# A graph network on one core: the spread of the last layer through all eight PSUM banks, with stores for two steps

## The chip, the cores and the metric

One Trainium2 chip, one of its cores. The metric is the time of one execution in device microseconds (us). A kernel is run several times and its median is given; one further execution is profiled.

## The reference

Four graph layers work on 12,500 nodes of 32 features and 400,000 edges (`src`, `dst`). After each one the features are `x = layernorm(x + layer(x))`. The layers are graph attention, a normalised partial convolution, a radial convolution with two spherical degrees, and a two-step graph convolution. The change concerns the last of them:

```python
def gcn_conv(x, W, b, row, col, n_nodes):
    xw = x @ W
    deg = segment_sum(ones, col); dinv = where(deg > 0, rsqrt(deg), 0)
    msgs = (dinv[row] * dinv[col])[:, None] * xw[row]
    return segment_sum(msgs, col, n_nodes) + b
...
h = relu(gcn_conv(x, W1, b1, row, col, n))      # row = src, col = dst, with a loop on each node
h = relu(gcn_conv(h, W2, b2, row, col, n))
```

So each of the two convolutions takes a row of 32 numbers per edge from its source node and adds it to its destination node.

## The kernel before

The node table lies in SBUF, 98 windows of 128 nodes. A gather of 400,000 single rows is avoided in this way. The edges are sorted by source, padded and cut into chunks of four edges. A **spread** multiplies a 0/1 matrix with the node table: for each edge slot its source row comes out, in three bf16 parts that sum to the fp32 row (3 x 32 = 96 columns for an edge, 384 for a chunk). The result goes to a DRAM table (`spread`) of chunks, 768 bytes each. Then a **collect** reads these chunks back in the order of the other end by indirect DMAs and sums them into the nodes. Layer 2 has a spread and a collect (k = 0, 34 features), the last layer has two of each (k = 1 and k = 2, 32 features), with small matrix products between them. Spread and collect follow each other: the collect reads what the spread wrote, anywhere in it.

A spread has 468 steps (`XSTEPS`), each of two groups of 128 chunks. The engines run their own loops and wait for each other by semaphores. For k = 1 and 2 a step n goes like this:

- SP loads the keys of four steps at once, 512 KB written to SBUF (4,096 bytes, the same ones, to each partition), into one of three key buffers (`key_load`).
- DVE makes the 0/1 matrix of the step, 128 x 1024 bf16, in `hotT` (`row_hot`, L2285). There are two such buffers; the matrix of step n + 2 waits until the matmuls of step n are done (`spread_raw`).
- PE runs eight matmuls of 96 columns (`spread_rows`, L1353) into two PSUM banks. Steps take turns between banks 0 and 1 and banks 2 and 3: step n waits until step n - 2 has been read (`spread_read`). PE's loop goes round every four steps, and each pair of steps loads its window numbers.
- ACT copies both banks as bf16 to one of four buffers in `srcs` (L1011), 1,536 bytes in a partition. It waits until the store of step n - 4 has landed (`spread_out`).
- SP stores the buffer, 128 runs of 1,536 bytes, 192 KB (L572). One queue, SP's, carries the key loads and the stores, in the order in which SP's program has them: the key load of a group of four stands ahead of the store of its fourth step.

Behind a spread, DVE clears the sums (L2311), and POOL begins the gathers of the collect once every store has landed. The chunk numbers by which it gathers are made long before, in `edge_list`, by shifts and masks: chunk (step n, partition p, group g) lies at row 256 n + 2 p + g.

For k = 0 the spread shares the copies between ACT and DVE, ACT's queue has the stores, and POOL gathers edge records meanwhile.

Of the kernel before, what the change touches and what calls it, by code (L numbers as in the profile page):

```python
# [7 lines left out]
BF16 = mybir.dt.bfloat16  # L8
I32 = mybir.dt.int32
U8 = mybir.dt.uint8  # L10
ALU = mybir.AluOpType
# [3 lines left out]
P = 128  # L15
# [17 lines left out]
SLOTS = 4  # L33
# [23 lines left out]
CHUNK_EDGES = 4  # L57
XTILES = CHUNK_EDGES
XGROUP = XTILES * P
XGPS = 2  # L60
XITERS = -(-((E + W * W * (CHUNK_EDGES - 1) + W * (XGROUP - CHUNK_EDGES)) // XGROUP) // (SLOTS * XGPS))
XSTEPS = XITERS * SLOTS
KEYS = 12
KEY_ITERS = XSTEPS // KEYS
RING = KEYS // SLOTS
assert KEY_ITERS * KEYS == XSTEPS and KEYS % SLOTS == 0
XG = XSTEPS * XGPS
XT = XG * XTILES
CHUNKS = XG * P
# [13 lines left out]
CHUNK_MASK = (1 << 17) - 1  # L83
# [74 lines left out]
def resnorm_gnn_kernel(nc, a, out):  # L158

    ctx = ExitStack()  # L160
    with ctx:
# [3 lines left out]
        def sem(name):  # L165
            return ctx.enter_context(nc.semaphore(name))
# [175 lines left out]
        def chunk_rows(s, c):  # L342
            size = XGPS * CHUNK_EDGES * 3 * c
            return srcs[:, s * size // 2:(s + 1) * size // 2].bitcast(BF16).rearrange("p (g c) -> p g c", g=XGPS)

        hotT_row = [hotT[:, b, :, :].rearrange("p t n -> p (t n)") for b in range(2)]

        yb = hot[:, :, :, :].rearrange("p b t n -> p (b t n)")[:, 0:2 * PW * P].rearrange("p (b w n) -> p b w n", b=2, w=PW)
# [53 lines left out]
        spread_read = sem("spread_read")  # L402
        spread_half = sem("spread_half")
        spread_out = [sem(f"spread_out{s}") for s in range(SLOTS)]
        nbx_in = [sem(f"nbx_in{r}") for r in range(RING)]
        chunks_in = [sem(f"chunks_in{s}") for s in range(SLOTS)]
        sq_in = sem("sq_in")
# [107 lines left out]
        def _(sp):  # L515
# [41 lines left out]

            def spread_moves(k, c, keys, rows):

                rows_v = rows.rearrange("(n p g) c -> p n g c", p=P, g=XGPS)  # L560
                keys_v = keys.rearrange("(m b) c -> m (b c)", b=SLOTS)

                def key_load(m, r):
                    sp.dma_start(row_keys_in[r], keys_v[bass.ds(m, 1), :].to_broadcast([P, SLOTS * XGPS * XGROUP])).then_inc(row_key_landed[r], 16)

                def step(i, s, final):
                    n = i * KEYS + s
                    if not final and s % SLOTS == SLOTS - 1:
                        sp.wait_ge(spread_hot, n + (k * XSTEPS + SLOTS + 1))
                        key_load(i * RING + (RING + s // SLOTS), s // SLOTS)  # L570
                    sp.wait_ge(spread_read, n + (k * XSTEPS + 3))
                    sp.dma_start(rows_v[:, bass.ds(n, 1), :, :],  # L572
                                 chunk_rows(s % SLOTS, c).rearrange("p (a g) c -> p a g c", a=1)).then_inc(spread_out[s % SLOTS], 16)

                for r in range(RING):
                    sp.wait_ge(spread_hot, k * XSTEPS + (SLOTS - KEYS + (r + 1) * SLOTS))
                    key_load(r, r)
                with sp.Fori(0, KEY_ITERS - 1) as i:
                    for s in range(KEYS):
                        step(i, s, False)  # L580
                for s in range(KEYS):
                    step(KEY_ITERS - 1, s, True)
# [97 lines left out]
            sp.wait_ge(row_keys_sent, 32)  # L680
            for s in range(SLOTS):
                sp.wait_ge(staged_out[s], 16 * ITERS)
                sp.wait_ge(spread_out[s], 16 * 3 * XITERS)

        N_LOADS = 18

# [2 lines left out]
        def _(pool):  # L689
# [99 lines left out]
                        gather_step(pas, i, s, False)  # L789

            def chunk_gather(k, pas, c, rows):
                for s in range(SLOTS):
                    pool.wait_ge(spread_out[s], 16 * XITERS * (k + 1))
                with pool.Fori(0, KEY_ITERS) as i:
                    for r in range(RING):
                        pool.wait_ge(nbx_in[r], i * 16 + (16 * k * KEY_ITERS + 16))
                        for s in range(SLOTS):
                            pool.wait_ge(sums_ready, i * KEYS + (SUMS_BASE[pas] + r * SLOTS + s + 1 - SLOTS))
                            pool.nop(nofuse=True)
                            for q in range(XGPS):  # L800
                                pool.indirect_dma_start(  # L801
                                    out=chunk_rows(s, c)[:, q, :], out_offset=None, in_=rows,
                                    in_offset=bass.IndirectOffsetOnAxis(ap=nbx[:, r, s * XGPS + q:s * XGPS + q + 1], axis=0),
                                ).then_inc(chunks_in[s], 16)
# [53 lines left out]
        def _(act):  # L858
# [136 lines left out]

            def spread_rows(k, c, keys, rows):
                c3 = 3 * c
                rows_v = rows.rearrange("(n p g) c -> p n g c", p=P, g=XGPS)
                keys_v = keys.rearrange("(m b) c -> m (b c)", b=SLOTS)

                def key_load(m, r):
                    act.dma_start(row_keys_in[r], keys_v[bass.ds(m, 1), :].to_broadcast([P, SLOTS * XGPS * XGROUP])).then_inc(row_key_landed[r], 16)

                def step(i, s, first, final):
                    n = i * KEYS + s
                    slot = s % SLOTS
                    act.wait_ge(spread_raw, n + (k * XSTEPS + 3))
                    if k or not first or s >= SLOTS:
                        act.wait_ge(spread_out[slot], i * (16 * KEYS // SLOTS) + 16 * (s // SLOTS + k * XITERS))
                    if k:  # L1010
                        s_.copy(chunk_rows(slot, c), banks[:, 2 * (s % 2):2 * (s % 2) + 2, 0:CHUNK_EDGES * c3]).then_inc(spread_read, 1)  # L1011
                        return
                    s_.copy(chunk_rows(slot, c)[:, 0, :], bank[2 * (s % 2)][:, 0:CHUNK_EDGES * c3]).then_inc(spread_read, 1)
                    act.wait_ge(spread_read, n + (k * XSTEPS + 3))
                    act.wait_ge(spread_half, n + 1)
                    act.dma_start(rows_v[:, bass.ds(n, 1), :, :],
                                  chunk_rows(slot, c).rearrange("p (a g) c -> p a g c", a=1)).then_inc(spread_out[slot], 16)
                    if not final and s % SLOTS == SLOTS - 1:
                        act.wait_ge(spread_hot, n + (k * XSTEPS + SLOTS + 1))
                        key_load(i * RING + (RING + s // SLOTS), s // SLOTS)  # L1020

                if k == 0:
                    for r in range(RING):
                        key_load(r, r)
                for s in range(KEYS):
                    step(0, s, True, False)
                with act.Fori(1, KEY_ITERS - 1) as i:
                    for s in range(KEYS):
                        step(i, s, False, False)
                for s in range(KEYS):  # L1030
                    step(KEY_ITERS - 1, s, False, True)
# [98 lines left out]
        def _(pe):  # L1130
# [209 lines left out]
            def spread_rows(k, c, win_tab):  # L1340
                c3 = 3 * c
                tabs = acc[:, 0:W * c3 // 2].bitcast(BF16)
                with pe.Fori(0, XITERS) as i:
                    for s in range(SLOTS):
                        n = i * SLOTS + s
                        if s % 2 == 0:
                            pair = group_windows(pe, PE_ENGINE, win_tab, i * (SLOTS // 2) + s // 2)
                        wins = pair[s % 2 * XGPS:(s % 2 + 1) * XGPS]
                        pe.wait_ge(spread_hot, n + (k * XSTEPS + SLOTS + 1))
                        pe.wait_ge(spread_read, n + (k * XSTEPS + 1))  # L1350
                        for q in range(XGPS):
                            for j in range(CHUNK_EDGES):
                                last = t_.matmul(bank[2 * (s % 2) + q][:, j * c3:(j + 1) * c3],  # L1353
                                                 hotT_row[s % 2][:, q * XGROUP + j:(q + 1) * XGROUP:CHUNK_EDGES],
                                                 tabs[:, bass.ds(wins[q] * c3, c3)], start=True, stop=True)
                        last.then_inc(spread_raw, 1)
# [89 lines left out]
        def _(dve):  # L1446
# [483 lines left out]
            def edge_list(k, ends, others, key_tab, numbers):  # L1930
# [17 lines left out]
                dve.drain()  # L1948
                wide = numbers.shape[1]
                low, high = [sortA[:, b * wide:(b + 1) * wide].bitcast(I32) for b in range(2)]  # L1950
                v.tensor_scalar(low, got, P - 1, 1, ALU.bitwise_and, ALU.logical_shift_left)
                v.tensor_scalar(high, got, CHUNK_MASK - (XGPS * P - 1), None, ALU.bitwise_and)
                v.tensor_scalar(numbers[:, :], got, 7, XGPS - 1, ALU.logical_shift_right, ALU.bitwise_and)
                dve.drain()
                v.tensor_tensor(low, low, high, ALU.bitwise_or)
                dve.drain()
# [308 lines left out]
            def spread_rows(k, c):  # L2265
# [33 lines left out]
                else:  # L2299
# [7 lines left out]
                            evict(i - 1 if s == 0 else i, (s - 1) % KEYS, False)  # L2307
                    evict(KEY_ITERS - 1, KEYS - 1, False)
                dve.wait_ge(spread_raw, (k + 1) * XSTEPS + 2)
                dve.drain()  # L2310
                v.memset(acc[:, 0:W * c3], 0.0)  # L2311
                dve.drain()
# [287 lines left out]
```

## Time and profile before

| | us |
|---|---|
| median of 3 runs (lowest, highest) | 19703.42 (19679.15, 19707.19) |
| the profiled execution | 19675.2 |
| its span, from first to last instruction | 19673.4 |
| spread k = 1, first matrix to last copy | 15917.7 to 16489.6 |
| spread k = 2, the same | 17838.8 to 18413.3 |

The profiled execution lies 28 us under the median and 4 us under the fastest of the three runs. Times in rows are from the span's start. Busy time is that of an engine's own work; "granted clock" (PEclk) is TensorE's, as a share of 2.4 GHz, and at any moment it is 0.50 or 1.00.

### The profile page before, as it was taken

The page shows a single profiled execution, that of the slowest core. Times are in us where ns is not written, and L with a number is a line of the kernel's source. Part 1 is how long each engine was busy: PE and PEld are TensorE (multiplying, and loading weights), DVE is VectorE, ACT ScalarE, POOL GpSimd, SP SyncE. Part 2 cuts the span into 40 slices and gives each one's busy share as a digit, 9 for nine tenths or more (in the row PEclk, how much of TensorE's full clock was granted, in tenths as well). Part 3 has the DMA queues.
Part 4 walks back from the last instruction along what each step waited for, and adds up shares of the span by engine and source line. Part 5 has one row for each costly group of instructions (what it writes and reads, how often), then busy time and mean ns, then how long its engine had stood idle before and what let it go on. Part 6 is the DMA issues. An engine that isn't in the chain of part 4 may idle for free.

```text
span 19673.4 us, 267135 instructions
## 1 busy us (share of the span) xinstructions
PE 9126.0 (46%) x63546; PEld 6808.2 (35%) x63547; DVE 16353.7 (83%) x22350; ACT 6238.3 (32%) x13799; POOL 12841.6 (65%) x13651
## 2 busy tenths in 40 slices
PE   0113101001016776603348887887888764327432
PEld 0113101001016665402235555555555543225322
DVE  9989999999998888816669999999999976665666
ACT  0001333333315553300015555555555553005200
POOL 0047777777777777777757777777777613760476
PEclk6556555555559997555568888888888855555555
DMA  1024444444422223713330000000001165245524
GB/s 19 0 56 31 32 34 32 33 30 32 33 26 59 48 48 87 244 31 84 84 39 13 13 13 13 13 13 13 13 13 13 12 174 177 79 72 196 159 79 69
DMA packets 1751554, 1095.95 MB, mean 56 GB/s; under 512 B 1217323, under 2 KB 1658124, under 8 KB 1750028
## 3 DMA queue, kind: packets, MB, share of 16 engines
q0 software_dynamic: 454272, 412.11, 17.5%
q1 hardware_dynamic: 1089532, 417.46, 8.5%
q10 hardware_dynamic: 207632, 265.14, 4.3%
q14 instruction: 84, 0.69, 0.0%
q8 instruction: 34, 0.56, 0.0%
HBM read 700.94 MB, written 391.12 MB: 56 GB/s over the span
## 4 chain that ended last, share of the span: by engine, by line
POOL 32%; DVE 25%; issue 16%; DMA 13%; DVEq 8%; PE 5%; ACT 1%; POOLq 0%; SPq 0%; ACTq 0%
POOL gat L779 16%; POOL pay L745 12%; DVE red L2504 12%; DMA srcs<-spread,nbx 9%; DVE srcs L2497 5%; DVEq L2503 4%; POOL srcs L801 4%; DMA spread<-srcs 3%; PE banks L1267 3%; DVE arena L1721 2%; DVE srcs L2493 2%; ACT srcs L1011 1%; DVEq L1791 1%; DVEq L2487 1%; PE banks L1353 1%
## 5 line engine op out<-in xcount | busy, mean ns | idle before, releaser
L779 POOL DMA_INDIRECT gat<-tab,nbr x3328 | 3330.8, 1001 | 2142.7 <-DMA nbr<-nbr_src 1128.6
L801 POOL DMA_INDIRECT srcs<-spread,nbx x2808 | 2655.2, 946 | 2305.0 <-DMA nbx<-from_src 1381.4
L779 POOL DMA_INDIRECT gat<-tab,pay x3328 | 3166.9, 952 | 1080.0 <-issue 816.2
L1411 PE MATMUL banks<-w2rows,dsts 128*128 128x384 f32 x6656 | 3030.9, 593 | 793.3 <-DVE srcs L2497 702.3
L745 POOL DMA_INDIRECT pay<-records,nbr x2560 | 2520.5, 985 | 795.3 <-issue 779.4
L1267 PE MATMUL banks<-srcs,hot 128*128 128x96 bf16 (+1 forms) x11232 | 1148.6, 279 | 2900.3 <-DMA srcs<-spread,nbx 2814.0
L2504 DVE TENSOR_REDUCE red<-srcs 128x160 f32<-128x2560 f32 x832 | 2346.3, 2820 | 75.8
L1196 PE MATMUL banks<-ident,arena 128*128 128x128 f32 x2240 | 429.8, 379 | 4206.5 <-DVE arena L1749 2792.2
L897 ACT COPY banks<-arena 128x1024 f32<-128x1024 f32 (+1 forms) x1508 | 1325.3, 880 | 2970.6 <-DVE arena L1749 1273.4
L2188 DVE TENSOR_TENSOR arena<-arena,banks 128x96 f32 (+2 forms) x2816 | 722.9, 257 | 1618.5 <-PE banks L1267 1344.0
L1267 PEld LDWEIGHTS banks<-srcs,hot 128*128 128x128 bf16 x11232 | 874.9, 134 | 3174.0 <-issue 1590.0
L1196 PEld LDWEIGHTS banks<-ident,arena 128*128 128x128 f32 x2240 | 404.1, 204 | 4232.7 <-DVE arena L1749 2802.5
L1411 PEld LDWEIGHTS banks<-w2rows,dsts 128*128 128x128 f32 x6656 | 1306.1, 218 | 1558.0 <-DVE srcs L2497 883.8
L2497 DVE TENSOR_TENSOR srcs<-banks,g_v 128x768 f32<-128x768 f32 x1664 | 1576.9, 948 | 0.0
L1748 DVE TENSOR_TENSOR arena<-banks,arena 128x1024 f32<-128x1024 f32 (+1 forms) x1508 | 1533.1, 1017 | 22.8 <-ACT banks L897 22.8
L1749 DVE TENSOR_TENSOR arena<-banks,arena 128x1024 f32<-128x1024 f32 (+1 forms) x1508 | 1532.8, 1016 | 0.0
L1353 PE MATMUL banks<-arena,hotT 128*128 x11232 | 1161.0, 282 | 757.5 <-DVE hotT L2285 347.2
L2285 DVE TENSOR_SCALAR hotT<-dsts,lanes 128x1024 bf16<-128x1024 uint8 x1404 | 1080.3, 775 | 447.4 <-PE banks L1353 426.7
L2493 DVE TENSOR_TENSOR srcs<-banks,g_s 128x512 f32<-128x512 f32 x1664 | 1142.1, 686 | 138.9 <-issue 63.2
L1353 PEld LDWEIGHTS banks<-arena,hotT 128*128 128x128 bf16 x11232 | 883.2, 139 | 1035.0 <-issue 1029.4
L1060 ACT COPY arena<-banks 128x57 f32 x1664 | 341.3, 205 | 2707.5 <-PE banks L1398 2682.1
L2177 DVE TENSOR_TENSOR hot<-banks,key_dst 128x1024 bf16<-128x1024 f32 x936 | 1141.2, 1219 | 38.6 <-issue 38.5
(383 smaller groups left out, 20253.1 us busy)
## 6 DMA issues: line engine op xcount, KB each, us to landing
spread<-srcs SPq DMA_DIRECT2D x936, 192.0 KB
dsts<-key_rows SPq DMA_DIRECT2D x234, 512.0 KB
spread<-srcs ACTq DMA_DIRECT2D x468, 204.0 KB
staged<-gat SPq DMA_DIRECT2D x416, 148.0 KB
gat<-staged ACTq DMA_DIRECT2D x416, 148.0 KB
dsts<-key_rows ACTq DMA_DIRECT2D x117, 512.0 KB
gat<-tab,nbr POOLq DMA_INDIRECT x3328
gat<-tab,pay POOLq DMA_INDIRECT x3328
```

What stands on the lines that cost most here:

```text
L745: pool.indirect_dma_start(out=pay[:, s, t, :], out_offset=None, in_=records, in_offset=bass.IndirectOffsetOnAxis(ap=nbr[:, s, t:t + 1], ax ...
L779: pool.indirect_dma_start(out=gatv(s, GC[pas])[:, t, :], out_offset=None, in_=TAB[pas], in_offset=bass.IndirectOffsetOnAxis(ap=row, axis=0 ...
L801: pool.indirect_dma_start(out=chunk_rows(s, c)[:, q, :], out_offset=None, in_=rows, in_offset=bass.IndirectOffsetOnAxis(ap=nbx[:, r, s * X ...
L897: s_.copy(sort_held(part, log, first), first).then_inc(operand_held, 1)
L1267: last = t_.matmul(where(q), hots[:, t, :], rows(t), start=(h == 0), stop=(h == tiles - 1))
L1353: last = t_.matmul(bank[2 * (s % 2) + q][:, j * c3:(j + 1) * c3], hotT_row[s % 2][:, q * XGROUP + j:(q + 1) * XGROUP:CHUNK_EDGES], tabs[:, ...
L1411: last = t_.matmul(bank[1 + 2 * (p % 2) + h][:, 0:384], hid_rows[:, s % 2, 2 * p + h, :], w2rows[:, :], start=True, stop=True)
L1748: v.tensor_tensor(b[:, d, e, :, :, :], held, a[:, d, 1, :, :, :], ALU.min)
L1749: last = v.tensor_tensor(b[:, d, 1 - e, :, :, :], held, a[:, d, 1, :, :, :], ALU.max)
L2493: v.tensor_tensor(prod[:, f0:f0 + 2, 0:16, :], banks[:, lo:lo + 2, 0:256].rearrange("p t (u k) -> p t u k", k=16), g_s[:, b, t0:t0 + 2, :] ...
L2497: v.tensor_tensor(prod[:, f0:f0 + 2, 16:40, :].rearrange("p t (o u) k -> p t o u k", o=3), banks[:, lo:lo + 2, 256:384].rearrange("p t (a ...
L2504: v.tensor_reduce(red[:, b, t0 - 2:t0 + 2, 0:40], prod[:, :, :, :], AX.X, ALU.add)
```

## The change

In the two spreads of the last layer (k = 1 and 2) the steps go round all eight PSUM banks, four pairs of them, so PE waits for the read of step n - 4 in place of n - 2. ACT copies into three pair buffers (`pair_rows`, in another part of SBUF, `acc`), each of which holds two steps: in a partition 3,072 bytes that follow each other. One store for two steps, 384 KB, takes the place of two stores of 192 KB. In DRAM the rows of two steps now lie side by side for a partition, chunk at row 512 (n // 2) + 4 p + 2 (n mod 2) + g, and `edge_list` makes chunk numbers for that, with as many instructions. The spread of k = 0 writes the same order of rows with its stores as they were, one for a step: 128 runs of 1,632 bytes, now 3,264 bytes apart. Before it clears the sums, DVE also waits for ACT's last copy. `hotT`, the key buffers and PE's loop stay as they are.

```diff
+PAIRS = 3
+SPREAD_DEEP = 4
+PAIR_USES = XSTEPS // 2 // PAIRS
...
+        def pair_rows(j, c):
+            size = 2 * XGPS * CHUNK_EDGES * 3 * c
+            return acc[:, 9600 + j * size // 2:9600 + (j + 1) * size // 2].bitcast(BF16).rearrange("p (a g c) -> p a g c", a=2, g=XGPS)
...
             def spread_moves(k, c, keys, rows):
-                rows_v = rows.rearrange("(n p g) c -> p n g c", p=P, g=XGPS)
+                rows_v = rows.rearrange("(n p a g) c -> p n (a g c)", p=P, a=2, g=XGPS)
...
-                    sp.wait_ge(spread_read, n + (k * XSTEPS + 3))
-                    sp.dma_start(rows_v[:, bass.ds(n, 1), :, :],
-                                 chunk_rows(s % SLOTS, c).rearrange("p (a g) c -> p a g c", a=1)).then_inc(spread_out[s % SLOTS], 16)
+                    if s % 2:
+                        j = s // 2 % PAIRS
+                        sp.wait_ge(spread_read, n + (k * XSTEPS + 3))
+                        sp.dma_start(rows_v[:, bass.ds(i * (KEYS // 2) + s // 2, 1), :],
+                                     pair_rows(j, c).rearrange("p a g c -> p (a g c)").rearrange("p (n c) -> p n c", n=1)).then_inc(pair_out[j], 16)
...
             def spread_rows(k, c, keys, rows):
                     act.wait_ge(spread_raw, n + (k * XSTEPS + 3))
-                    if k or not first or s >= SLOTS:
-                        act.wait_ge(spread_out[slot], i * (16 * KEYS // SLOTS) + 16 * (s // SLOTS + k * XITERS))
                     if k:
-                        s_.copy(chunk_rows(slot, c), banks[:, 2 * (s % 2):2 * (s % 2) + 2, 0:CHUNK_EDGES * c3]).then_inc(spread_read, 1)
+                        j, used = s // 2 % PAIRS, s // 2 // PAIRS + (k - 1) * PAIR_USES
+                        if s % 2 == 0 and (used or not first):
+                            act.wait_ge(pair_out[j], i * (16 * KEYS // 2 // PAIRS) + 16 * used)
+                        s_.copy(pair_rows(j, c)[:, s % 2, :, :], banks[:, 2 * (s % SPREAD_DEEP):2 * (s % SPREAD_DEEP) + 2, 0:CHUNK_EDGES * c3]).then_inc(spread_read, 1)
                         return
...
-                    act.dma_start(rows_v[:, bass.ds(n, 1), :, :],
+                    act.dma_start(rows_v[:, bass.ds(i * (KEYS // 2) + s // 2, 1), s % 2, :, :],
...
             def spread_rows(k, c, win_tab):
-                        pe.wait_ge(spread_read, n + (k * XSTEPS + 1))
+                        deep = SPREAD_DEEP if k else 2
+                        pe.wait_ge(spread_read, n + (k * XSTEPS + 3 - deep))
...
-                                last = t_.matmul(bank[2 * (s % 2) + q][:, j * c3:(j + 1) * c3],
+                                last = t_.matmul(bank[2 * (s % deep) + q][:, j * c3:(j + 1) * c3],
...
-                v.tensor_scalar(low, got, P - 1, 1, ALU.bitwise_and, ALU.logical_shift_left)
-                v.tensor_scalar(high, got, CHUNK_MASK - (XGPS * P - 1), None, ALU.bitwise_and)
-                v.tensor_scalar(numbers[:, :], got, 7, XGPS - 1, ALU.logical_shift_right, ALU.bitwise_and)
+                v.tensor_scalar(low, got, P - 1, 2, ALU.bitwise_and, ALU.logical_shift_left)
+                v.tensor_scalar(high, got, CHUNK_MASK - (2 * XGPS * P - 1), None, ALU.bitwise_and)
+                v.tensor_scalar(numbers[:, :], got, 7, 2 * XGPS - 1, ALU.logical_shift_right, ALU.bitwise_and)
...
                 dve.wait_ge(spread_raw, (k + 1) * XSTEPS + 2)
+                dve.wait_ge(spread_read, (k + 1) * XSTEPS + 2)
                 dve.drain()
                 v.memset(acc[:, 0:W * c3], 0.0)
```

The program orders of the two engines that the stores tie together show the change. First ACT, in its loop over twelve steps of a spread of the last layer, a few copies from the loop's start on (`srcs` and `arena` are where the copy writes; what a copy waits for stands behind it). Before:

```order
L1011 CAST srcs<-banks 128x768 [waits spread_out0]
L1007 REGISTER_ALU
L1011 CAST srcs<-banks 128x768 [waits spread_out1,spread_raw]
L1007 REGISTER_ALU
L1011 CAST srcs<-banks 128x768 [waits spread_out2,spread_raw]
L1007 REGISTER_ALU
L1011 CAST srcs<-banks 128x768 [waits spread_out3,spread_raw]
L1007 REGISTER_ALU
L1009 REGISTER_ALU [waits spread_raw]
L1011 CAST srcs<-banks 128x768 [waits spread_out0]
```

and now:

```order
L1030 CAST arena<-banks 128x768 [waits pair_out0]
L1025 REGISTER_ALU
L1030 CAST arena<-banks 128x768 [waits spread_raw]
L1025 REGISTER_ALU
L1030 CAST arena<-banks 128x768 [waits pair_out1,spread_raw]
L1025 REGISTER_ALU
L1030 CAST arena<-banks 128x768 [waits spread_raw]
L1025 REGISTER_ALU
L1030 CAST arena<-banks 128x768 [waits pair_out2,spread_raw]
L1025 REGISTER_ALU
L1030 CAST arena<-banks 128x768 [waits spread_raw]
```

Every copy waited for a store of its own slot; now every second one waits for the store of a pair, three pairs back.

Second SP, in the same loop, around a key load (`dsts` is the key buffer). Before:

```order
L572 ISA [waits spread_read]
L572 DMA spread<-srcs 128x768
L569 REGISTER_ALU
L564 ISA [waits spread_hot]
L564 DMA dsts<-key_rows 128x4096
L571 REGISTER_ALU
L572 ISA [waits spread_read]
L572 DMA spread<-srcs 128x768
L571 REGISTER_ALU
L572 ISA [waits spread_read]
L572 DMA spread<-srcs 128x768
```

and now:

```order
L584 ISA [waits spread_read]
L584 DMA spread<-arena 128x1536
L579 REGISTER_ALU
L574 ISA [waits spread_hot]
L574 DMA dsts<-key_rows 128x4096
L583 REGISTER_ALU
L584 ISA [waits spread_read]
L584 DMA spread<-arena 128x1536
L584 ISA [waits spread_read]
L584 DMA spread<-arena 128x1536
```

The key load stood ahead of the fourth store of four; it now stands ahead of the second of two, so it comes up in SP's program right behind the store of the first two steps, and the store that follows it waits for two more copies.

## Rows read from the trace of the kernel before

**Rows 1.** First spread, busy us of PE, PEld, DVE, ACT, POOL; PEclk, DMA share, GB/s.

```profile
15917.70:16489.60 571.90, 377.29 (x3744) 289.25 (x3744) 348.35 (x468) 362.60 (x468) 0.00 (x0) 0.50 0.79 265
```

**Rows 2.** ACT's copies (L1011), first spread, then second: durations, first and last start; idle before.

```profile
L1011 ACT CAST srcs<-banks x468: 798/798/809, 15919.5 to 16488.8; 128x768 bf16<-128x768 f32 x156
  DMA spread<-srcs: 118.2, 86
...
L1011 ACT CAST srcs<-banks x468: 798/798/809, 17840.7 to 18412.5; 128x768 bf16<-128x768 f32 x156
```

**Rows 3.** Who waited for whom, 15925 to 16480: us in total, times, longest.

```profile
PE banks L1353 <- ACT srcs L1011: 162.4, 213, 1.8
...
PE banks L1353 <- DVE hotT L2285: 2.6, 3, 1.0
```

**Rows 4.** The chain of waits, 15925 to 16480, by line.

```profile
by line: DMA spread<-srcs 60.2%; ACT srcs L1011 17.2%; PE banks L1353 12.3%; issue 6.4%; SPq L572 2.4%; SPq L564 1.4%; ACTq L1009 0.3%; SPq L571 0.1%; SPq L569 0.1%
```

**Rows 5.** The same chain in order of time, from 16201: start, us, what.

```profile
16201.93 4.36 DMA spread<-srcs
...
16206.36 0.81 ACT srcs L1011
...
16211.52 0.81 ACT srcs L1011
...
16212.49 2.93 DMA spread<-srcs
...
16221.55 4.31 DMA spread<-srcs
```

**Rows 6.** PE in order of time at the spread's start: start, us, [idle before <-releaser].

```profile
15918.67 1.48 PE L1353 MATMUL banks<-arena,hotT 128*128 x16 [43.84 <-DVE hotT L2285]
15920.52 1.49 PE L1353 MATMUL banks<-arena,hotT 128*128 x16 [0.36 <-ACT srcs L1011]
15922.62 1.47 PE L1353 MATMUL banks<-arena,hotT 128*128 x16 [0.61 <-ACT srcs L1011]
15924.47 1.49 PE L1353 MATMUL banks<-arena,hotT 128*128 x16 [0.39 <-ACT srcs L1011]
```

**Rows 7.** PE's weight loads and DVE's matrices in order of time, from 16201.

```profile
16201.89 0.61 PEld L1353 LDWEIGHTS banks<-arena,hotT 128*128 128x128 bf16 x8 [1.15 <-issue]
16202.76 0.75 DVE L2285 TENSOR_SCALAR hotT<-dsts,lanes 128x1024 bf16<-128x1024 uint8 x1 [1.02 <-PE banks L1353]
16203.74 0.62 PEld L1353 LDWEIGHTS banks<-arena,hotT 128*128 128x128 bf16 x8 [0.28 <-issue]
16205.23 0.62 PEld L1353 LDWEIGHTS banks<-arena,hotT 128*128 128x128 bf16 x8 [0.87 <-issue]
```

**Rows 8.** DMA queue of SP, 15925 to 16480: packets, MB, share of 16 engines; issues.

```profile
q1 hardware_dynamic: 81635, 148.69, 80.3%
spread<-srcs SPq DMA_DIRECT2D x454, 192.0 KB
```

**Rows 9.** The same queue, 15921.2 to 15923.1, in which two stores and nothing else move.

```profile
q1 hardware_dynamic: 288, 0.39, 58.3%
```

**Rows 10.** The same queue, 15875.1 to 15881.3, in which three key loads and nothing else move.

```profile
q1 hardware_dynamic: 432, 1.57, 68.5%
```

**Rows 11.** Busy time by engine in two stretches of the first spread, columns as in rows 1.

```profile
16166.00:16170.00 4.00, 2.98 (x32) 2.49 (x32) 2.79 (x4) 2.92 (x4) 0.00 (x0) 0.50 0.79 247
16170.00:16173.00 3.00, 1.07 (x17) 0.81 (x16) 1.56 (x3) 1.62 (x3) 0.00 (x0) 1.00 0.94 308
```

**Rows 12.** From spread to collect, all engines in order of time.

```profile
16488.12 1.50 ACT L1011 CAST srcs<-banks 128x768 bf16<-128x768 f32 x2 [0.35 <-PE banks L1353]
16490.88 7.90 DVE L2311 MEMSET arena<- 128x9408 f32 x1 [3.19 <-issue]
16492.87 0.98 POOL L801 DMA_INDIRECT srcs<-spread,nbx  x1 [651.11 <-DMA nbx<-from_src]
```

**Rows 13.** The chain of waits during layer 2's spread (k = 0), 7700 to 8600, by line.

```profile
by line: POOL pay L745 75.6%; issue 23.8%; POOLq L743 0.3%; POOLq L751 0.2%; POOLq L742 0.1%
```

More of the change, by code:

```diff
@@ L66 @@
 assert KEY_ITERS * KEYS == XSTEPS and KEYS % SLOTS == 0
+PAIRS = 3
+SPREAD_DEEP = 4
+assert SLOTS % SPREAD_DEEP == 0
+PAIR_USES = XSTEPS // 2 // PAIRS
+assert KEYS % (2 * PAIRS) == 0 and PAIR_USES * PAIRS * 2 == XSTEPS
 XG = XSTEPS * XGPS
@@ L404, in resnorm_gnn_kernel @@
         spread_out = [sem(f"spread_out{s}") for s in range(SLOTS)]
+        pair_out = [sem(f"pair_out{j}") for j in range(PAIRS)]
         nbx_in = [sem(f"nbx_in{r}") for r in range(RING)]
@@ L682, in _ @@
                 sp.wait_ge(staged_out[s], 16 * ITERS)
-                sp.wait_ge(spread_out[s], 16 * 3 * XITERS)
+                sp.wait_ge(spread_out[s], 16 * XITERS)
+            for j in range(PAIRS):
+                sp.wait_ge(pair_out[j], 16 * 2 * PAIR_USES)
         N_LOADS = 18
@@ L791, in chunk_gather @@
             def chunk_gather(k, pas, c, rows):
-                for s in range(SLOTS):
-                    pool.wait_ge(spread_out[s], 16 * XITERS * (k + 1))
+                if k:
+                    for j in range(PAIRS):
+                        pool.wait_ge(pair_out[j], 16 * PAIR_USES * k)
+                else:
+                    for s in range(SLOTS):
+                        pool.wait_ge(spread_out[s], 16 * XITERS)
                 with pool.Fori(0, KEY_ITERS) as i:
@@ L997, in spread_rows @@
                 c3 = 3 * c
-                rows_v = rows.rearrange("(n p g) c -> p n g c", p=P, g=XGPS)
+                rows_v = rows.rearrange("(n p a g) c -> p n a g c", p=P, a=2, g=XGPS)
                 keys_v = keys.rearrange("(m b) c -> m (b c)", b=SLOTS)
@@ L1007, in step @@
                     act.wait_ge(spread_raw, n + (k * XSTEPS + 3))
-                    if k or not first or s >= SLOTS:
-                        act.wait_ge(spread_out[slot], i * (16 * KEYS // SLOTS) + 16 * (s // SLOTS + k * XITERS))
                     if k:
-                        s_.copy(chunk_rows(slot, c), banks[:, 2 * (s % 2):2 * (s % 2) + 2, 0:CHUNK_EDGES * c3]).then_inc(spread_read, 1)
+                        j, used = s // 2 % PAIRS, s // 2 // PAIRS + (k - 1) * PAIR_USES
+                        if s % 2 == 0 and (used or not first):
+                            act.wait_ge(pair_out[j], i * (16 * KEYS // 2 // PAIRS) + 16 * used)
+                        s_.copy(pair_rows(j, c)[:, s % 2, :, :], banks[:, 2 * (s % SPREAD_DEEP):2 * (s % SPREAD_DEEP) + 2, 0:CHUNK_EDGES * c3]).then_inc(spread_read, 1)
                         return
+                    if not first or s >= SLOTS:
+                        act.wait_ge(spread_out[slot], i * (16 * KEYS // SLOTS) + 16 * (s // SLOTS))
                     s_.copy(chunk_rows(slot, c)[:, 0, :], bank[2 * (s % 2)][:, 0:CHUNK_EDGES * c3]).then_inc(spread_read, 1)
```

## The prediction

> **What bounds the kernel now.** I read the busy time by stretch first, to see whether an engine is full in the two spreads that the change touches. In the first [rows 1] none is: of 571.9 us PE is busy for 377.3, ACT for 362.6, DVE for 348.4, and the 16 DMA engines for 0.79 of the time. TensorE's granted clock is 0.50, its lower level. The group of ACT's copies [rows 2] gives the step: 467 intervals in 15919.5 to 16488.8 and 467 in 17840.7 to 18412.5, 569.3 + 571.8 = 1141.1 us for 934, so 1.22 us a step, where the copy itself takes 0.80. ACT sits idle for 118.2 us of the first spread until a store has landed. The waits [rows 3] say that PE in turn waits for ACT (162.4 us) and almost never for DVE's matrix (2.6). The chain of waits [rows 4] puts the weight: 60.2% of it is stores in flight.
>
> The chain in order of time [rows 5] shows the ring that this makes. A copy begins 0.07 us after the landing it waited for (16206.29 to 16206.36), takes 0.80, and its store starts 0.16 later (a copy ends at 16212.33, the store is issued at 16212.49) and lands after 4.36, 2.93 or 4.31 us. With the mean of these, 3.87, four buffers go round in 0.07 + 0.80 + 0.16 + 3.87 = 4.90 us, 1.22 a step: the step that was read off. So the ring of four store buffers sets the pace, and the depth and the landing of stores are what counts.
>
> **The change part by part.** Three other limits lie below the 1.22, and the new step is set by the highest of them and of the new ring.
>
> *The new ring.* Three pairs are six steps. One turn: two copies in a row (1.50 [rows 12]), 0.16 to the issue, the landing, and 0.07. The landing grows by what the second half adds on the DMA engines: two stores alone take 0.583 of 1.9 us [rows 9], 0.55 us each. From 2.93, 3.87 and 4.36 that makes 3.48, 4.42 and 4.91, turns of 5.21, 6.15 and 6.64 us, and 0.87, **1.03** and 1.11 a step. I take the middle, since the mean of the same rows gave the present step to the second digit. One thing speaks for less: the key load now comes up in SP's program before the two copies that the next store waits for, so it can run while they are made. Another for more: the engines will have less idle time, so queues are longer. I let them cancel.
>
> *The loop of DVE and PE.* `hotT` stays two deep. A step's weight loads start at 16201.89, DVE begins the matrix that reuses its buffer at 16202.76, takes 0.75, and PE starts on it at 16203.74 [rows 7]: 1.85 us for two steps, 0.93 a step. At the spread's start, when no store is late yet, PE's pairs start at 15918.67, 15920.52, 15922.62 and 15924.47 [rows 6]: gaps of 1.85, 2.10 and 1.85. The 1.85 is the matrix loop; the 2.10 is where PE's program goes round (PE's weight loads idle 0.87 us there, against 0.28 between steps inside [rows 7]). Four steps in 3.95, **0.99** a step, is what the program runs at when stores do not hold it, between 0.93 and 0.99 if deeper banks shorten the turn.
>
> *The banks by themselves.* PE's waits for ACT in rows 6 are 0.36 and 0.39 us in front of pairs that come 1.85 after the pair before, the matrix loop's own time: without the wait for ACT there would be one for the matrix. I count the eight banks at nothing of their own. What they do is to let PE and DVE run two steps further while ACT is held, so that a late store costs ACT's spare time and not theirs; this work hides the ring's unevenness. Were it gone, the step would lie between 1.03 and the 1.11 of the late landings.
>
> The Trainium skill ("Perfetto Trace Analysis", section Matmul Optimizations) asks that all eight PSUM banks be used, for the sake of instruction-level parallelism. Taken by itself it would let the whole wait of PE for ACT go, 162.4 us in 454 of 468 steps, 167 a spread and 335 in all, and the kernel would come to 19368. Rows 6 speak against that, and the sum by them is the one below; it stays as a rival.
>
> *The DMA engines.* In 555 us they work for 0.803 of the time, on 454 stores and their keys [rows 8]: 0.98 us a step. A store alone is 0.55, so a key load in the mixed stream is 4 x (0.98 - 0.55) = 1.71; alone it is 0.685 x 6.2 / 3 = 1.42 [rows 10]. A pair store is not in the trace. Above, two stores: 1.11. Below, the key load's price per byte, 384 / 512 x 1.42 = 1.06, since its runs are longer (4,096 bytes against 1,536; the new ones have 3,072). I take 1.08. Four steps: 1.71 + 2 x 1.08 = 3.87, **0.97** a step; with the ends 0.89 and 0.98. The longer runs thus save hardly anything; the halved number of stores on SP's queue saves SP, which nobody waits for.
>
> *What lies at nothing.* Chunk numbers: the same instructions with other constants. DVE's wait for the last copy: that ends at 16489.62, and DVE clears the sums only from 16490.88 [rows 12], 1.26 us later, by an idle time in which it waits for nothing that the profile shows. If that cover were gone it would cost 0.83 us a spread. Behind it stands the collect's first matrix, not the gathers. Stores of k = 0: as many runs of the same size, in other places; if they took longer, POOL's gathers of edge records hide it, which are the chain of that time [rows 13], and without that cover 10% on a store of 0.55 would be 0.06 us a step. *At the end* of a spread the last store moves 0.55 us more before POOL may start: 1.1 us in two.
>
> **Sum.** The highest limit is the ring, 1.03. 934 x 1.03 = 962.0, and 1141.1 - 962.0 = 179.1, less 1.1, is 178.0 us. The profiled execution, 19675.2, becomes 19497. The median of the runs lies 28.2 over the profiled execution, so it becomes 19703.4 - 178.0 = 19525.
>
> **The rivals.**
>
> *A. The DMA engines are full at the share they have.* For it: the share is 0.79 to 0.80 throughout, with a ring that is only a little too slow. Against it: 0.94 in a stretch of 3 us [rows 11]. If 0.80 were the ceiling, the step would be 0.97 / 0.80 = 1.21: 9 us saved, 19695. If it lay a little higher, at 0.83, 1.17: 50 us, 19654.
>
> *B. The ring's late landings rule*, because pairs must wait for the slowest: 1.11 a step, 103 us saved, 19600.
>
> *C. The ring is no limit, and the clock rises.* Denser matmuls could raise TensorE's clock. It did so once in the first spread: after a stretch of 32 matmuls at 0.50 came one at 1.00, in which 16 matmuls took 1.07 us, 0.53 a step [rows 11], where 16 took 1.48 before [rows 6]. Then the matrix loop falls by some 0.3 in 1.85, and with the key load run early the step is that of the DMA engines, 0.97 down to 0.93: 234 to 271 us saved, 19432 to 19469. Against it: the stretch at 15918.67 was as dense and the clock stayed [rows 6, 1]. The Trainium skill ("TensorE: Matmul & The Clock Gate", section What's actually happening) has the throttled clock as the default and activity as what releases it; the two rows of rows 11 agree.
>
> *D. The banks alone give the gain* that PE's wait promises: 0.86 a step, 335 us, 19368. It needs the ring at its best (0.87) and the matrix loop below its 0.93.
>
> *E. Slower: the pair store waits behind more.* A turn of six steps takes longer than now if the landing exceeds 6 x 1.22 - 1.73 = 5.6 us. If each pair store had one more key load and one more pair store ahead of it than the quickest of rows 5, it would land after 2.93 + 0.55 + 1.71 + 1.08 = 6.3 us, a turn would take 8.0, a step 1.33: 105 us more, 19808. Against it: the DMA engines are idle for a fifth of the time, and the longest of rows 5 becomes 4.91, under the point that decides.
>
> **How the numbers follow.** Chances: my forecast (0.98 to 1.07 a step) 0.56; A 0.11, B 0.10, C 0.14, D 0.04, E 0.05. The range runs from C's better end to past B and leaves out D, E and most of A: 19430 to 19630. A measurement of this kernel tells about 0.2% (39 us) from no change. Faster by more: the forecast, B, C, D and half of A, 0.89; within it: the other half, 0.06; slower: 0.05.
>
> **What would show it.** In the profile after, the copies should come at 1.03 us; ACT's idle until a store has landed should fall from 118 us to under 50 a spread, PE's wait for ACT to near zero, and in their place PE should wait for DVE's matrix. The DMA share should rise to 0.94. A store should land 3.5 to 4.9 us after its issue. I am wrong if the share stays at 0.80 with a step above 1.15 (A), if the granted clock is often 1.00 (C), if stores land later than 5.6 us (E), or if the time of the collects changes: I found nothing that would move them.

## The result and the profile after

| us | before | after |
|---|---|---|
| median of the runs, 3 before, 4 after (lowest, highest) | 19703.42 (19679.15, 19707.19) | 19579.28 (19547.84, 19586.15) |
| the profiled execution (after, one of the four runs) | 19675.2 | 19547.8 |
| a step of the first spread, of the second | 1.219, 1.224 | 1.089, 1.088 |

The change makes the kernel faster: ratio 0.9935, 95% interval 0.9924 to 0.9947, 124.1 us less. The prediction was 19525 in a range of 19430 to 19630: the sign and the range hold, the saving was forecast at 178. A step, here and below, is the time from the first to the last start of ACT's copies in a spread, divided by 467.

The copies of the changed kernel, first spread and second, with ACT's idle time before them (us, times), answer to [rows 2]:

```profile
L1030 ACT CAST arena<-banks x468: 798/806/885, 15913.4 to 16422.1; 128x768 bf16<-128x768 f32 x156
...
  DMA spread<-arena: 144.5, 100
  PE banks L1375: 42.0, 19
...
L1030 ACT CAST arena<-banks x468: 798/806/885, 17775.3 to 18283.6; 128x768 bf16<-128x768 f32 x156
```

508.7 and 508.3 us for 467 steps. Before it was 569.3 and 571.8, so 124.1 us are gone here, as much as the medians differ. But ACT's idle time until a store has landed did not fall from 118.2 us to under 50: it rose to 144.5. The stretch of the first spread, columns as in [rows 1], and of the collect behind it:

```profile
15911.50:16422.90 511.40, 343.64 (x3744) 285.96 (x3744) 333.79 (x468) 340.24 (x468) 0.00 (x0) 0.52 0.87 296
16422.90:17644.00 1221.10, 376.35 (x3744) 286.55 (x3744) 797.86 (x1411) 0.07 (x1) 884.61 (x936) 0.50 0.37 76
```

The DMA share is 0.87, not 0.94. The collect took 1222.4 us before (16489.6 to 17712.0), so nothing moved there. Who waited for whom in this spread, 15925 to 16420, answers to [rows 3]:

```profile
DVE hotT L2307 <- PE banks L1375: 167.9, 219, 1.5
ACT arena L1030 <- DMA spread<-arena: 143.8, 99, 2.3
PE banks L1375 <- ACT arena L1030: 93.2, 107, 1.6
PE banks L1375 <- DVE hotT L2307: 68.7, 121, 1.3
```

PE's wait for ACT fell from 162.4 to 93.2 us, its wait for DVE's matrix rose from 2.6 to 68.7. Both moved as forecast, neither far enough: stores still set the pace. The queue of SP in the same stretch (packets, MB, share; issues, KB, median us to landing) answers to [rows 8]:

```profile
q1 hardware_dynamic: 48672, 147.60, 87.4%
...
spread<-arena SPq DMA_DIRECT2D x226, 384.0 KB, 4.6
```

495 us x 0.874 / (2 x 226) is 0.957 us of DMA work a step. The chain of waits from 16194 on (start, us, what) answers to [rows 5]:

```profile
16194.75 5.45 DMA spread<-arena
16200.22 0.04 ACT arena L1030
16200.92 0.26 ACT arena L1030
16201.61 1.53 ACT arena L1030 x2
16203.30 5.59 DMA spread<-arena
16208.97 0.05 ACT arena L1030
16209.67 0.19 ACT arena L1030
16210.36 1.53 ACT arena L1030 x2
16212.07 5.66 DMA spread<-arena
```

One turn is landing, four copies in a row, next store: 16203.30 to 16212.07, 8.77 us for eight steps, 1.096 a step. The landings on these rows are 5.4 to 5.7 us, where the prediction had 3.48 to 4.91; the median of all 226 stores, 4.6, lies inside that, but the long ones are those that hold ACT.

### The profile page after: what moved, and what is told of

Same layout as the page of the kernel before. It is cut to its first block, busy times and chain, and to the rows that moved or that the text cites. A ratio compares the mean times of both kernels' runs of the same rounds, so it can differ in the third digit from the quotient of the medians.

```text
span 19545.8 us, 264830 instructions
## 1 busy us (share of the span) xinstructions
PE 9058.4 (46%) x63546; PEld 6806.2 (35%) x63547; DVE 16324.0 (84%) x22350; ACT 6194.7 (32%) x13799; POOL 12837.3 (66%) x13651
## 4 chain that ended last, share of the span: by engine, by line
POOL 33%; DVE 25%; issue 16%; DMA 13%; DVEq 8%; PE 5%; ACT 1%; POOLq 0%; ACTq 0%; SPq 0%
POOL gat L793 17%; POOL pay L759 12%; DVE red L2527 12%; DMA srcs<-spread,nbx 9%; DVE srcs L2520 5%; DVEq L2526 4%; POOL srcs L819 4%; DMA spread<-arena 3%; PE banks L1288 3%; DVE arena L1743 2%; DVE srcs L2516 2%; ACT arena L1030 1%; DVEq L1813 1%; DVEq L2510 1%; DVE g_s L2511 1%
## 5 line engine op out<-in xcount | busy, mean ns | idle before, releaser
L1375 PE MATMUL banks<-arena,hotT 128*128 x11232 | 1091.4, 279 | 703.2 <-DVE hotT L2307 492.8
```

The source lines that it names most:

```text
L1375: last = t_.matmul(bank[2 * (s % deep) + q][:, j * c3:(j + 1) * c3], hotT_row[s % 2][:, q * XGROUP + j:(q + 1) * XGROUP:CHUNK_EDGES], tabs ...
```

## The experiments

In the expectations R is the account on record: the ring of store buffers sets the pace, before and after. B is that the banks make the gain, E that the DMA engines are full at their share. These letters are not those of the prediction's rivals. Names of other rivals are told where they stand. Every kernel was timed beside the kernel before on its chip (medians 19688.58 for the first four below, e1 to e4; 19684.82 for e5, e6, e8 and e9; 19681.30 for e10 to e12).

| kernel | median us | ratio to before, 95% | step, first and second spread |
|---|---|---|---|
| e1 before, eight banks | 19610.12 | 0.9962 [0.9948, 0.9975] | 1.151, 1.148 |
| e2 changed, four banks | 19556.01 | 0.9934 [0.9921, 0.9948] | 1.084, 1.086 |
| e3 changed, six pairs | 19446.64 | 0.9875 [0.9860, 0.9891] | 0.958, 0.967 |
| e4 changed, key loads on ACT's queue | 19663.14 | 0.9988 [0.9979, 0.9997] | 1.200, 1.200 |
| e5 changed, six single stores | 19529.30 | 0.9921 [0.9907, 0.9934] | 1.067, 1.061 |
| e6 changed, small key loads | 19450.12 | 0.9881 [0.9866, 0.9896] | 0.979, 0.980 |
| e8 six pairs, four banks | 19453.03 | 0.9881 [0.9866, 0.9897] | 0.966, 0.979 |
| e9 changed, key load behind the store | 19561.17 | 0.9936 [0.9922, 0.9949] | 1.096, 1.095 |
| e10 six pairs, DVE's wait later | 19439.27 | 0.9878 [0.9862, 0.9893] | 0.965, 0.969 |
| e11 changed, two pairs | 19592.58 | 0.9956 [0.9943, 0.9970] | 1.131, 1.127 |
| e12 twelve single stores | 19482.25 | 0.9898 [0.9883, 0.9913] | 1.011, 1.006 |

The spreads explain every time to within 11 us: 934 x (1.2217 - step) gives 67 us for e1 (78 measured), 242 for e3 (242), 199 for e12 (199).

**How many buffers (e3, e11).** Three more pairs lie where the four single buffers were; e11 has two.

```diff
-PAIRS = 3
+PAIRS = 6
...
-            return acc[:, 9600 + j * size // 2:9600 + (j + 1) * size // 2].bitcast(BF16).rearrange("p (a g c) -> p a g c", a=2, g=XGPS)
+            part, at = (acc, 9600 + j * size // 2) if j < 3 else (srcs, (j - 3) * size // 2)
+            return part[:, at:at + size // 2].bitcast(BF16).rearrange("p (a g c) -> p a g c", a=2, g=XGPS)
```

> The changed kernel with six pair buffers, three in the old place of the copies and three in the new, all else as it is. R: the ring is twelve steps round and no limit; the step falls to that of the loop of DVE and PE or of the DMA engines' own work, 0.96 to 1.01 us, 19460 to 19505. Rival E (engines): the DMA engines at their share of 0.87 are as full as this traffic gets them, so the step stays 1.06 to 1.09, 19550 to 19580.

The step is 0.96. Waits of e3, 15950 to 16350, and its stretch (columns as in [rows 1]):

```profile
DVE hotT L2308 <- PE banks L1376: 100.5, 191, 1.0
PE banks L1376 <- ACT srcs L1031: 52.2, 96, 1.2
ACT arena L1031 <- PE banks L1376: 47.4, 95, 1.0
```

```profile
15950.00:16350.00 400.00, 284.33 (x3334) 236.20 (x3332) 296.38 (x418) 313.21 (x418) 0.00 (x0) 0.62 0.95 342
```

No copy waits for a store any more; DVE, PE and ACT wait for each other. The engines work 0.95 of the time, so 0.87 was no ceiling: E is out. The ring held the changed kernel. TensorE's granted clock has a small part in the 0.96. Two stretches of e3:

```profile
16250.00:16290.00 40.00, 30.30 (x330) 25.67 (x331) 29.16 (x42) 30.89 (x42) 0.00 (x0) 0.50 0.94 341
16010.00:16050.00 40.00, 26.14 (x336) 21.32 (x336) 30.69 (x44) 32.36 (x44) 0.00 (x0) 0.74 0.98 349
```

At a clock of 0.50 throughout, 42 copies start between 16249.4 and 16288.9, 0.96 a step (0.985 from 16310 to 16350, at 0.50 too); at a mean of 0.74, 44 start between 16009.6 and 16049.4, 0.93.

> The changed kernel with two pair buffers in place of three: four steps of buffers as before the change, with the merged stores and eight banks. Theory R (the number of buffers sets the pace, and merging by itself costs, since a store joins the queue only when both halves are copied): a turn of four steps is 1.50 + 0.23 + a landing of 4.0 to 5.0 = 5.7 to 6.7, 1.43 to 1.68 a step, so 190 to 430 us slower than before the change, 19880 to 20120. Rival M (stores for two steps with longer runs are themselves the gain): at or under the step of eight banks alone, 1.15, 19560 to 19625.

Rival M's numbers came: 1.13 a step and 19592.58, 0.02 a step under eight banks with single stores (e1). R's 1.43 to 1.68 is far off: its landing of 4.0 to 5.0 was far too long. That merged stores are the gain does not follow, though, as the next two kernels show. The chain of waits of e11, and its queue from 15950 to 16350:

```profile
16202.06 2.31 DMA spread<-arena
...
16206.12 3.25 DMA spread<-arena
...
16211.12 2.65 DMA spread<-arena
...
16215.54 2.79 DMA spread<-arena
...
16220.08 2.97 DMA spread<-arena
```

```profile
q1 hardware_dynamic: 38129, 115.67, 83.1%
...
spread<-arena SPq DMA_DIRECT2D x177, 384.0 KB, 2.6
```

A turn of four steps is 4.50 us (16202.06 to 16220.08, four turns). The prediction's formula for a turn holds: 1.73 for copies and issue and the mean landing of these rows, 2.79, make 4.52. With three pairs six steps of 1.089 leave 6.53 - 1.73 = 4.80 for it. The medians of all stores, 2.6 and 4.6, differ by as much. So a third pair adds 2.0 us to the landing, about the DMA work of the two more steps in flight, 2 x 0.957 = 1.9. Most of what a deeper ring gives is taken back by a longer landing; only the rest, 4.52 / 4 against 6.53 / 6, is gained. With six pairs the loop would let a landing take 12 x 0.96 - 1.73 = 9.8 us, and the medians are 4.6 and 5.3: the ring is out of it.

**Merged or single (e5, e12).** Each half of a pair buffer is stored as soon as it is copied, and ACT waits for each half's own store. e12 does this to e3's kernel.

```diff
-                    if s % 2:
-                        j = s // 2 % PAIRS
-                        sp.wait_ge(spread_read, n + (k * XSTEPS + 3))
-                        sp.dma_start(rows_v[:, bass.ds(i * (KEYS // 2) + s // 2, 1), :],
-                                     pair_rows(j, c).rearrange("p a g c -> p (a g c)").rearrange("p (n c) -> p n c", n=1)).then_inc(pair_out[j], 16)
+                    j = s // 2 % PAIRS
+                    sp.wait_ge(spread_read, n + (k * XSTEPS + 3))
+                    sp.dma_start(rows_v[:, bass.ds(i * (KEYS // 2) + s // 2, 1), s % 2, :, :],
+                                 pair_rows(j, c)[:, s % 2:s % 2 + 1, :, :]).then_inc((pair_out, half_out)[s % 2][j], 16)
```

> The changed kernel with one store of 192 KB for each step in place of one of 384 KB for two, from the same three pair buffers, whose halves now are waited for singly: six buffers in the memory of three pairs. The order of rows in DRAM stays, so the runs are 1,536 bytes, 3,072 apart. Theory R (the number of steps that may be in flight sets the pace, and a merged store is late because it joins the queue only when both halves are copied): a turn of six steps is one copy 0.80, 0.23 to the issue and back, and a landing of 3.9 as before the change, 4.9 us, 0.82 a step, which is no limit; the step falls to 0.96 to 1.01, 19480 to 19520. Theory M (the merged store and its longer runs are what the change gains by, the depth little): without them the step goes back towards the one before, 1.12 to 1.20, 19610 to 19680.

1.06, short of both. A single store lands after 4.9 us (median), no sooner than a merged one (4.6). I take it that four copies in a burst put the same work into the queue; no run separates that. And DVE now waits for keys. Waits of e5, 15950 to 16350:

```profile
ACT arena L1032 <- DMA spread<-arena: 107.6, 81, 2.4
...
DVE hotT L2309 <- DMA dsts<-key_rows: 54.2, 59, 2.1
```

> Six pair buffers whose halves are stored singly, 192 KB for each step: twelve buffers, nothing merged. Theory R (depth is what counts): no copy waits for a store, the step is that of the loop of PE and DVE, 0.96 to 0.99, 19440 to 19480. Rival M (with single stores the DMA engines or SP's queue become the bound, as the share was 0.91 with six single buffers and DVE waited for keys): the step stays at 1.03 to 1.07, 19510 to 19550.

1.01, again between. No copy waits for a store in e12. The step is 0.04 to 0.05 longer than with merged stores (e3). From 15950 to 16350 key loads are 4.5% of the chain, and the DMA engines work 400 x 0.967 / 394 = 0.98 us a step, against 400 x 0.953 / 418 = 0.91 in e3. That this work makes the step longer fits, but was not tested by itself. With six steps of buffers single stores are 0.025 a step better, with four (e1 against e11, which differ in the order of rows too) merged ones 0.02. So merging by itself is worth -0.025 to 0.05 a step, by the depth of the ring.

**The banks (e1, e2, e8).** e1 is the kernel before with eight banks and with DVE's added wait for the last copy; e2 and e8 are the changed kernel and that of six pairs with `SPREAD_DEEP = 2`.

```diff
-        banks[:, 2 * (s % 2):2 * (s % 2) + 2, 0:CHUNK_EDGES * c3]
+        banks[:, 2 * (s % SPREAD_DEEP):2 * (s % SPREAD_DEEP) + 2, 0:CHUNK_EDGES * c3]
...
-                        pe.wait_ge(spread_read, n + (k * XSTEPS + 1))
+                        deep = SPREAD_DEEP if k else 2
+                        pe.wait_ge(spread_read, n + (k * XSTEPS + 3 - deep))
```

> The kernel before with one edit alone: the steps of the last layer's spreads go round all eight PSUM banks; four single buffers, single stores as before. Theory R (ring): the step is set by how a buffer goes round, through the landing of a store that stands behind a key load; the ring of four single buffers is untouched, so the step stays 1.20 to 1.22 us and the time 19683 to 19703. Rival B (banks): what the change gained came from the banks; then the step is near 1.09 and the time near 19580.

Wrong for R: 78 us, more than half of the change's saving; B's 1.09 was not reached either. The chain of e1 by line, 15950 to 16350, and in time:

```profile
by line: DMA spread<-srcs 70.3%; ACT srcs L1012 17.3%; issue 7.2%; SPq L573 2.5%; PE banks L1355 2.0%; SPq L565 0.7%; ACTq L1010 0.4%; DVE hotT L2287 0.4%; ACTq L1008 0.2%; SPq L572 0.1%; SPq L570 0.1%; SPq L579 0.0%
```

```profile
16201.35 4.12 DMA spread<-srcs
16205.54 0.81 ACT srcs L1012
16206.51 3.84 DMA spread<-srcs
```

Before, PE's matmuls held 12.3% of the chain [rows 4]; here 2.0%. With two steps more in PSUM, ACT copies four times in a row when a store lands, and the ring runs alone: 4 x 1.15 = 4.60, which leaves 4.60 - 1.03 = 3.57 for the landing (3.84 and 4.12 in these rows; the mean of the 76 landings on this chain is 3.70).

> The changed kernel with PSUM two steps deep as before, pairs and merged stores kept. R: the turn of eight steps keeps its landing of some 5.6 us, and its four copies take 3.4 to 3.8 us in place of 3.05, since PE can be only two steps ahead: 1.10 to 1.16 a step, 19590 to 19645. B: back to 1.22, 19703.

> Six pair buffers (three more of them where the single ones lay), with PE going round four banks as before the change, two steps deep. Theory R (once no store is waited for, DVE's matrix buffers set the pace, and these are two deep however many banks there are): the step stays within 0.02 of the 0.96 of six pairs with eight banks, 19430 to 19470. Rival D2 (with the ring out of the way the banks are the next limit, as the copies then wait for PE and PE for the copies): the step goes back to 1.02 or more, 19500 or more.

In e2 neither R's 1.10 to 1.16 nor B's 1.22 came; in e8 R's numbers did. Both steps stay at those of the same buffers with eight banks (1.085 against 1.089; 0.966 and 0.979 against 0.958 and 0.967), and the intervals of the ratios overlap. In e2 PE is in the chain with 18.8%, but the median landing is 4.2 us in place of 4.6: what the banks give by bursts, the longer landing seems to take back. The Trainium skill ("Perfetto Trace Analysis", section Matmul Optimizations) wants all eight banks used: 78 us here on a ring of four, nothing measurable on three pairs or six, and in no case the 335 of the prediction's rival D. Counted in the order banks (e1), pairs (e11), third pair (changed), the step goes 1.222, 1.150, 1.129, 1.089, but e2 has the last without the banks: the shares depend on the order.

**What makes a landing long (e4, e9, e6).** e4 issues the loop's key loads from ACT's queue, behind the copy; e9 puts them behind the store of the fourth step in SP's program; e6 cuts them to 16 partitions.

```diff
-                    if not final and s % SLOTS == SLOTS - 1:
-                        sp.wait_ge(spread_hot, n + (k * XSTEPS + SLOTS + 1))
-                        key_load(i * RING + (RING + s // SLOTS), s // SLOTS)
...
+                        if not final and s % SLOTS == SLOTS - 1:
+                            act.wait_ge(spread_hot, n + (k * XSTEPS + SLOTS + 1))
+                            key_load(i * RING + (RING + s // SLOTS), s // SLOTS)
```

> The changed kernel with three pairs, but the key loads of the loop are issued by ACT behind its copy of each fourth step, on ACT's own DMA queue, so that no store stands behind a key load in its queue. R: the landing that the ring waits for falls from 5.6 us to 3.0 to 4.5, the step to 0.98 to 1.03, 19480 to 19525. E: the same bytes go through the same engines, 1.06 to 1.09, 19550 to 19580.

R's guess fell, and E's too: the stores land later, not earlier. Queues of e4, 15950 to 16350 (q10 is ACT's), and its chain in time:

```profile
q10 hardware_dynamic: 11872, 43.24, 42.1%
q1 hardware_dynamic: 23674, 64.65, 41.2%
...
spread<-arena SPq DMA_DIRECT2D x165, 384.0 KB, 5.8
```

```profile
16201.45 6.50 DMA spread<-arena
...
16211.11 6.42 DMA spread<-arena
```

A store that is alone on its queue lands no sooner for it; I read this as the key load's work on the same engines. The Trainium skill ("DMA: Bandwidth & Descriptors", section Issuing engines are not separate DMA queues) says that DMAs of all issuing engines run on the same 16 engines and interleave; the trace agrees (42.1% and 41.2% add up to the 0.83 that the 16 engines are busy), and shows the move dearer than neutral: 1.200 a step against 1.089. Why it is dearer was not told apart from the time that ACT itself spends on issuing (3.6% of the chain from 16200 to 16235).

> The changed kernel with each key load behind the store of its group's last two steps in SP's program, not ahead of it. Theory R (the engines' work in flight sets the landing, not the place in the queue): the store that was late now has its way free but the next one has the key load ahead of it; some landing of each four steps is long as before and the step stays at 1.06 to 1.10, 19555 to 19590. Rival P (the key load's place ahead of the store is what makes it late, since store, key load and store then come in one burst): the landing falls to about 4, the step to 0.97 to 1.03, 19470 to 19525.

Theory R's number: 1.096; DVE now also waits 77.7 of the 400 us for keys. But the edit did not take the burst away. SP's issues in e9:

```profile
16199.88 0.33 SPq L581 DMA_DIRECT2D spread<-arena  x1
16200.46 0.35 SPq L574 DMA_DIRECT2D dsts<-key_rows  x1
16201.28 0.33 SPq L581 DMA_DIRECT2D spread<-arena  x1
```

Store, key load and store still come within 1.4 us; the key load has only changed places among the stores. So e9 shows that it does not matter behind which of the two stores the key load stands. Whether a key load outside the burst would help, rival P's point, stays open.

> The changed kernel with the key loads of the loop cut to 16 of 128 partitions. It leaves out seven eighths of the key writes, so the other partitions make their matrices from keys of earlier steps; every instruction and every store stays. Theory R (a store's landing is the DMA work that is in flight with it, 3.8 us for two stores and a key load, 1.7 of it the key load): the landing behind the key load falls from 5.6 to about 4.1, eight steps from 8.77 to 7.3 us, below the loop of PE and DVE; the step falls to 0.95 to 1.01, 19465 to 19520. Rival Q (a landing is mostly a fixed time, the key load has little part in it): the step stays at 1.06 to 1.09, 19550 to 19590.

R: 0.98. Queue of e6, 15950 to 16350:

```profile
q1 hardware_dynamic: 32727, 87.11, 61.0%
...
spread<-arena SPq DMA_DIRECT2D x205, 384.0 KB, 2.4
```

The same stores, the same ring of three pairs, and the landing is 2.4 in place of 4.6 us, with the stores off the chain (DMA holds 0.7% of it). So with most of the key bytes gone 2.2 of the 4.6 us go: about half of a landing was the key loads' work beside it. With the engines at 0.61 the step is no shorter than with six pairs at 0.95: 0.96 to 0.98 is the loop of DVE, PE and ACT.

**DVE's wait for the last copy (e10).** In e3's kernel the added wait stands behind the clearing of the sums.

```diff
                 dve.wait_ge(spread_raw, (k + 1) * XSTEPS + 2)
-                dve.wait_ge(spread_read, (k + 1) * XSTEPS + 2)
                 dve.drain()
                 v.memset(acc[:, 0:W * c3], 0.0)
+                dve.wait_ge(spread_read, (k + 1) * XSTEPS + 2)
```

> Six pair buffers, with DVE's wait for the last copy behind the clearing of the sums and not ahead of it. Theory W (the wait is what delays the clearing, since nothing covered it): the clearing starts some 1.2 us earlier in a spread against the last matrix, as in the kernel before; in the time that is 2.4 us of 19447, not to be told from none, so the profile decides. Rival: the clearing starts as late as with the wait, as it is delayed by something else. Time by both: 19430 to 19465.

The clearing in the changed kernel, in e3 and in e10, with DVE's idle time before it in brackets; before the change it was 3.19 [rows 12]:

```profile
16425.13 7.90 DVE L2334 MEMSET arena<- 128x9408 f32 x1 [4.33 <-issue]
```

```profile
16375.09 7.90 DVE L2335 MEMSET arena<- 128x9408 f32 x1 [4.14 <-issue]
```

```profile
16377.45 7.90 DVE L2334 MEMSET arena<- 128x9408 f32 x1 [3.19 <-issue]
```

So the wait delays the clearing by 1.14 us in the changed kernel's first spread (1.37 in the second, 4.53 against 3.16), and moving it gives 0.95 back. In the time this can't be seen. e3 and e10 are the fastest kernels of the study, 1.2% under the kernel before.

## Why the prediction came near, and where it was off

- **The ring sets the pace, before and after:** right. e3 takes the wait for stores away and the step falls to 0.96.
- **The new ring, 1.03 a step:** this is the term that was mis-sized. It measured 1.089, and 934 x (1.0888 - 1.03) = 54.9 us is all of the miss between 179.1 and 124.1. The form of the turn holds for two pairs (4.52 against 4.50 in e11). In the changed kernel the chain goes round by eight steps, four copies and a landing of 5.6; put into the prediction's form, 1.73 and a landing for six steps, it leaves 4.80 where "the landing grows by what the second half adds" had 4.42. The 4.80 is what is left over, not a landing that was read. Two errors lie in it. 12.3% of the old chain was PE [rows 4], which my formula left out, so the 3.87 that closed the old sum was no measure of the ring alone: e1, where PE is 2.0% of the chain, leaves 3.57. And from there the growth was 1.23 and not 0.55: a landing grows by all the work that the deeper ring puts in flight beside it (2.0 us for the third pair in e11's comparison). It was luck that the first error hid 0.30 of the second's 0.68.
- **"I let them cancel":** the key load gets hardly any time to itself. Copies come in bursts, and store, key load and store reach the queue within 1.4 us (issues at 16201.90, 16202.49 and 16203.30). The other of the two, longer queues, was the one that held.
- **The loop of DVE and PE, 0.93 to 0.99:** right, 0.96 to 0.98 in e3, e6, e8 and e10, at clocks of 0.56 to 0.62 in their first spreads; 0.96 and 0.985 in e3 where the clock was 0.50.
- **"The banks by themselves" at nothing:** wrong for the ring of four (78 us in e1), on top of the pairs the nothing came true (e2), for another reason than the one given. It was read off the spread's start [rows 6], where no store was late yet; the gain comes behind a late store.
- **The DMA engines, 0.97 a step:** right, 0.957. The share came to 0.87 because the step is longer.
- **DVE's wait, "hidden":** wrong, by 1.14 and 1.37 us in the two spreads. The idle time that was to hide it starts when DVE's wait ends, so it moves with it.
- **The rivals:** A and its ceiling of 0.80 are out (0.87, and 0.95 in e3). B's number, 1.11, was nearest, for another reason than the slowest of the old landings. D is out by e1. E's point, a landing of 5.6 us, was reached by the store that gates each second burst, but the mean that a turn pays is 4.80. C is not what the change did, but it is what six pairs do: 19446.64, in C's 19432 to 19469, with a granted clock of 0.62, though at 0.50 the step is hardly longer.

## What to carry to other kernels

The landing of a store is not a constant to be carried into a deeper ring: with the DMA engines near full much of it is the work in flight: the third pair took its median from 2.6 to 4.6 us. With six pairs it grew little more (4.6 and 5.3), since the compute loop then set the pace. So size a ring by two bounds, the engines' work a step and the compute loop's step, and add buffers until a turn has some microseconds to spare; half-way, much of the gain is taken back. A gain of one part (here the banks) may lie in the same slack as that of another, so such parts don't add up.

## What the runs showed of the hardware that was not expected

A 384 KB store from the same buffers landed after 2.4 (e6), 2.6 (e11), 4.6 (changed) and 5.8 us (e4, median each), by what else was in flight. Moving the key loads to another queue made stores land 1.2 us later. TensorE's granted clock rose for short stretches in the kernels whose PE was held less by stores: its mean is 0.50 before, 0.52 in the changed kernel, 0.62 in e3, where 16 matmuls took 0.97 us at one place and 1.53 at another.
